# Second attention layer: the four product blocks of a sheet issued in three groups instead of four

## The reference, cut to what matters

```python
for ci in range(n_chunks):                      # chunks of 64 queries
    s = ci * chunk_size
    e = min(s + chunk_size, T)
    scores = jnp.einsum('bhtd,bhsd->bhts', q[:, :, s:e], k[:, :, :e]) * scale
    probs = jax.nn.softmax(scores, axis=-1)
    ...
    probs = probs * (0.5 + 0.5 * fhn_gate)      # a gate from the row's sum of probabilities
    probs = probs / (probs.sum(axis=-1, keepdims=True) + 1e-08)
    out_chunks.append(jnp.einsum('bhts,bhsd->bhtd', probs, v[:, :, :e]))
```

## Time and profile before

| | us |
|---|---|
| median of 3 runs | 1532.0 (1529.15 to 1532.43) |
| the profiled execution, its own time | 1530.86 |
| its span, first to last instruction | 1529.0 |
| second layer's stage, from the first scores (L2004) | 816.1 to the end |
| TensorE matmul busy | 1415.1 (93%) |
| VectorE busy | 1179.3 (77%) |
| ScalarE busy | 818.9 (54%) |
| GpSimd busy | 524.4 (34%) |

### The profile page before, as it was taken

How to read it: one execution, slowest core, us unless ns; L and a number is a source line. 1 busy time by engine, 2 the same in 40 slices (tenths; PEclk the granted TensorE clock), 3 DMA queues, 4 the chain that set the end, 5 groups by cost and what they waited for, 6 DMA issues and landing times.

```text
span 1529.0 us, 35462 instructions
## 1 busy us (share of the span) xinstructions
PE 1415.1 (93%) x12938; PEld 914.1 (60%) x12952; DVE 1179.3 (77%) x2690; ACT 818.9 (54%) x1565; POOL 524.4 (34%) x943
## 2 busy tenths in 40 slices
PE   3899999999998799999998999999999999999994
PEld 1667667667677699998885444444444444444432
DVE  3899889889888496456677788888888888888752
ACT  2344434534533333334434677777667777776672
POOL 2343333333233011162412244444444444442121
PEclk8899999999998899999999999999999999999996
DMA  4111111111111566776974343343344443432300
GB/s 121 40 42 56 47 40 58 45 42 56 38 37 36 160 211 209 213 249 209 269 201 78 91 104 99 93 105 93 85 102 105 103 101 94 104 89 71 81 9 14
DMA packets 119084, 152.86 MB, mean 100 GB/s; under 512 B 31348, under 2 KB 83700, under 8 KB 114292
## 3 DMA queue, kind: packets, MB, share of 16 engines
q1 hardware_dynamic: 105992, 120.25, 28.9%
q0 software_dynamic: 12928, 30.43, 6.9%
HBM read 109.01 MB, written 41.09 MB: 98 GB/s over the span
## 4 chain that ended last, share of the span: by engine, by line
PE 49%; DVE 32%; POOL 6%; issue 5%; ACT 5%; SPq 2%; DMA 1%; POOLq 0%; DVEq 0%; ACTq 0%
PE bank L1935 8%; PE bank L1926 8%; DVE P L1198 8%; DVE nmax L1503 8%; PE bank L1803 5%; PE bank L1981 5%; PE bank L2004 4%; ACT P L939 3%; PE bank L1760 2%; PE bank L1837 2%; PE bank L1944 2%; PE bank L1851 2%; DVE t L1073 1%; DVE t L1071 1%; PE bank L2051 1%
## 5 line engine op out<-in xcount | busy, mean ns | idle before, releaser
L1503 DVE TENSOR_REDUCE nmax<-bank 128x1 f32<-128x512 f32 (+3 forms) x704 | 428.6, 633 | 87.7 <-PE bank L1981 86.9
L939 ACT ACTIVATE P<-bank 128x512 f32<-128x512 f32 x640 | 371.3, 599 | 186.0 <-PE bank L2004 179.8
L1981 PE MATMUL bank<-KT,QT 76*128 76x512 bf16 (+3 forms) x1024 | 252.2, 304 | 28.8 <-DVE nmax L1503 20.4
L2004 PE MATMUL bank<-QT,KT 78*128 78x512 bf16 (+3 forms) x1024 | 246.1, 303 | 9.0 <-ACT P L939 5.6
L687 POOL DMA_INDIRECT xs_d<-xn,idx x128 | 124.5, 972 | 308.0 <-PE bank L1760 218.5
L1981 PEld LDWEIGHTS bank<-KT,QT 76*128 76x128 bf16 x1024 | 87.4, 97 | 188.2 <-DVE nmax L1503 129.4
L1803 PE MATMUL bank<-P,V 128*32 128x512 f32 (+3 forms) x2048 | 193.1, 450 | 0.0
L1198 DVE TENSOR_TENSOR P<-bank,early_w 128x512 f32<-128x512 f32 x256 | 158.6, 680 | 37.9 <-PE bank L1760 37.8
L903 ACT ACTIVATE hr<-bank 128x512 f32<-128x512 f32 x144 | 86.0, 597 | 177.9 <-PE bank L1926 174.9
L735 POOL DMA_INDIRECT hT<-ys_d,idx x104 | 103.5, 995 | 162.4 <-PE bank L2004 133.8
L1467 DVE TENSOR_TENSOR hT<-hr 128x512 f32<-128x512 f32 x144 | 98.0, 691 | 68.3 <-ACT hr L903 67.6
(11 more groups left out here) (257 smaller groups left out, 2227.2 us busy)
## 6 DMA issues: line engine op xcount, KB each, us to landing
P<-in_fc SPq DMA_DIRECT2D x72, 256.0 KB, 2.9
P<-in_proj SPq DMA_DIRECT2D x72, 256.0 KB, 3.5
QT<-parts_d SPq DMA_DIRECT2D x96, 192.0 KB
parts_d<-parts SPq DMA_DIRECT2D x32, 384.0 KB, 2.7
P<-xs_d SPq DMA_DIRECT2D x72, 128.0 KB, 3.0
ys_d<-P POOLq DMA_DIRECT2D x72, 128.0 KB, 3.6
KT<-parts_d SPq DMA_DIRECT2D x64, 128.0 KB
KT<-parts_d SPq DMA_DIRECT2D x32, 192.0 KB
```

Source lines behind the costliest of these rows:

```text
L939: nc.scalar.activation(P[s % 2][:, u, :], bank[k % 2][:, :], ACT.Exp, scale=float(DH) ** -0.5).then_inc(s_sb, 1)
L1503: nc.vector.tensor_reduce(nmax[:, s // TWO, h:h + TWO * nh - 1:TWO, j], max_bank(n, k)[:, 0:nh * w].rearrange("p (h w) -> p h w", h=nh), A ...
L1981: ins = pe.matmul(max_bank(n, k)[:, i * w:(i + 1) * w], QT[n.p][0:MROWS, h, j * 128:(j + 1) * 128], KT[n.p][0:MROWS, h, 0:w], start=True, ...
L2004: ins = pe.matmul(bank[k % 2][:, c:c + n], KT[b.p][0:SROWS, h, 128 * kb:128 * kb + 128], QT[b.p][0:SROWS, h, 128 * kb:T], start=True, stop ...
```

## The change

Three of the four blocks move or stay as follows: k = 0 stays behind unit 1, k = 1 goes from unit 3 to unit 4, k = 2 goes from unit 5 to unit 7, directly ahead of k = 3, which stays. Same instructions, same order among the blocks, same waits.

```diff
@@ -89,6 +89,7 @@
 PV_ORDER = [(0, G), (1, 2 * G), (3, 2 * G), (2, UNITS)]
+PV_AT = {1: (0,), 4: (1,), 7: (2, 3)}
 PLACE = {(g, kb): (u, c) for u in range(UNITS) for g, kb, c in unit_parts(u)}
@@ -2107,10 +2108,11 @@
                         maxes(2 if u == EXTRA else 1)
                         if core:
                             shifted_scores(b, s, u)
-                        if u in (1, 3, 5, 7) and s == 0 and before_:
-                            pv(b + -1, SHEETS - 1, u // 2)
-                        if u in (1, 3, 5, 7) and s > 0 and core:
-                            pv(b, s - 1, u // 2)
+                        for k in PV_AT.get(u, ()):
+                            if s == 0 and before_:
+                                pv(b + -1, SHEETS - 1, k)
+                            if s > 0 and core:
+                                pv(b, s - 1, k)
                         if where == (0, 1) and core:
                             r_rows(b)
```

## The result

The changed kernel takes 1548.11 us (median of 4 runs, 1547.29 to 1552.64), the kernel before 1532.22 (4 runs, 1529.15 to 1533.01). The ratio is 1.0116, 95% interval 1.0095 to 1.0138. The medians lie 15.9 us apart; by the ratio it is 17.8 us (14.6 to 21.1). Forecast was 1538.5, 6.5 us above the kernel before, and 1543.5 was the upper end. The direction was right; the forecast rise was less than half of the measured one.

What follows compares the result with a forecast made beforehand. A closed loop per batch passes between GpSimd's gate chain, VectorE, TensorE and ScalarE; 0.22 us in pass 0 plus 0.27 in pass 1 over 13 batches, plus ends, made 7.1 us: 1538.5 us, +0.4%, range 1531.5 to 1543.5.

Steps and rivals of the forecast that it cites:

- The price of a block: TensorE's product blocks: 0.21 us per 128 columns plus constants 0.14 and 0.09; joined pair taken at 0.79 us, at most 0.93.
- rival 4: Joined blocks: joining saves nothing, giving the upper bound of 1543.5 us; counted inside the main case, no chance of its own.
- k = 2 leaves unit 5, k = 1 goes to unit 4 in pass 1: Pass 1: -0.45 us for k = 2, a new 0.50 us stall at unit 4's second maximum for k = 1.
- k = 2 joins k = 3, pass 0: Block behind unit 7 grows by 0.22 us, delaying ScalarE's copy, the exponential of (0,8) and the scores of (1,0).
- Pass 2: Beside GpSimd's gate chain, covered by 1.30 us of slack: cost nothing, up to 0.3 us if that cover were gone.
- Period: Time per batch: 44.07 us instead of 43.58, from 0.22 in pass 0 plus 0.27 in pass 1.
- The whole part: Total of the summed terms over all batches: 13 x 0.49 = 6.4 us, 7.1 with first and last batches.
- Every sign that I had named for the changed profile: Joined block 0.79 us to next start, 0.5 us wait at (1,4), copy 0.22 later, tanh 0.49 later, batch 44.07.
- Pass 3: (3,5) and (3,6) delayed by 0.7 and 0.3 us, unnoticed by full VectorE; cost 0 to 0.1 us, taken as 0.
- so no term below is one of clock: All four passes: TensorE's granted clock is 1.00, its upper level of 2.4 GHz, so no clock term was counted.
- The bounds: Whole kernel: upper 1543.5 us with the joined pair at 0.93; lower about 1535 with the unit 4 stall at 0.25.
- The first rival: TensorE bounds throughout, each of 64 joined pairs returns 0.23 us: -14.7 us, 1517, or 1529 from pass 1 only; chance 0.12.

Runs made afterwards that it cites:

- e10: Kernel before, with k = 2 moved from unit 5 to unit 7 in pass 3 alone, k = 1 left behind unit 3; ratio 1.0050 to the kernel before.
- e3: Kernel before, with k = 2 joined to k = 3 behind unit 7 in all passes, k = 1 left behind unit 3; ratio 1.0031 to the kernel before.
- e1: Changed kernel with pass 3 alone put back as before; ratio 1.0038 to the kernel before.
- e2: Kernel before with pass 3 alone as in the changed kernel; ratio 1.0043 to the kernel before.
- e5: Changed kernel with the matmul of the first maximum of (3,4) issued five times, four matmuls more per batch; ratio 1.0025 to the kernel before.
- e11: Kernel before, with k = 1 moved from unit 3 to unit 4 in pass 3 alone, k = 2 left behind unit 5; ratio 1.0180 to the kernel before.
- e4: Kernel before, with k = 1 moved from unit 3 to unit 4 in all passes, nothing joined; ratio 1.0124 to the kernel before.
- e6: Kernel before, with k = 1 moved to unit 4 in pass 0, k = 2 joined to k = 3 in pass 1; ratio 0.9945 to the kernel before.
- e7: As e6, with the matmul of the first maximum of (3,4) issued three times; ratio 0.9985 to the kernel before.

## Why the prediction was right in direction and wrong in size

*The price of a block*: right. 0.79 us for the joined pair (1106.37 to 1107.16 in the changed kernel, 1182.81 to 1183.60 in e10); rival 4 falls.

*k = 2 leaves unit 5, k = 1 goes to unit 4 in pass 1*: right. Predicted a stall of 0.50 and +0.27 in pass 1; measured 0.51 and +0.29 ((1,3) to (1,8) of the changed kernel, 0.43 - 0.14).

*k = 2 joins k = 3, pass 0*: +0.22 predicted for joining, +0.22 measured (e3); in the changed kernel +0.14, because the moved k = 1 gives 0.08 ahead of it, a term that I left out.

*Pass 2*: right, beside the gate's chain; VectorE's idle time behind GpSimd went from 1.30 to 1.20 us.

*Period*: 44.07 predicted, 44.05 measured. That close is partly luck: 0.08 too much in pass 0, 0.02 too little in pass 1 and 0.04 more between (1,8) and (3,1), which I had at nothing, nearly cancel. The whole part, 7.1 us in the sum, measured 5.8 by the ratio (3.2 to 8.3, e1). Every sign that I had named for the changed profile came, and none of them looked at the clock.

*Pass 3*: the step that failed, with the sentence at its head, that the clock was 1.00 in all passes, "so no term below is one of clock". I walked pass 3 for delays alone, and these were right: (3,5) and (3,6) come 0.73 and 0.23 us later in e2, 0.7 and 0.3 were forecast. The wait at (3,4) is there in the working ("waits for VectorE anyway, 0.57 us"), not that it would grow, and I costed it at nothing since VectorE leads. It does cost nothing in time at full clock (e2: 43.58). But it moved 0.79 us of TensorE's work out of a stretch in which the engine was already waiting, its wait grew from 0.57 to 1.06 us with another 0.27 ahead of it, and in five of twelve batches the granted clock then fell to 0.50. At half clock TensorE becomes the bound of pass 3: 10.3 of the 15.7 us. The bounds had no such term, so the range ended at 1543.5. e1 takes the falls away by undoing pass 3 alone, e2 brings them back by changing pass 3 alone, and e5 has none after giving TensorE work in the wait without undoing the change.

*The first rival*, and with it the Trainium skill's rule (TensorEngine Tiling (Array Packing), Key Properties, changing the tiling mode drains TensorE): the trace agrees that a change of form costs about 0.23 us, and e3's pass 1 gained 0.28 from one pair fewer. What it does not give is the time of the kernel: of four passes only pass 1 can cash it.

What stays open: why the fall comes in some batches (every second in e2, every third from batch 1 on in e11) and not in each, when the undisturbed batches are alike to a few hundredths of a us; why e4 showed one fall and e11, with the same pass 3, four; why e6 gains more than its period; and how much of e5's gain over the changed kernel is the chip's.

## What to carry to other kernels

Work that fills an engine's wait is not free to move, even if the wait is on nobody's path: before moving matmuls out of a stretch in which TensorE already idles, add up what TensorE still does there, and carry a fall of the clock as a term of its own in the range. A granted clock of 1.00 before the change, as here, is no promise that it stays. Place work per stage, not by one rule for all: joining gained 0.28 us in pass 1 and lost 0.22 in pass 0, moving gained 0.08 in pass 0 and lost 0.57 in pass 1, and of the placements tried only a choice pass by pass (e6, e7) beat the kernel before.

## What the runs showed of the hardware that I had not expected

A kernel with four more matmuls in each batch was some 14 us faster against its kernel before (1.0025 instead of 1.0116, on two sets of rounds), and its granted clock stayed at 1.00 in batches 1 to 13. And moving 0.36 us of work out of a stretch that TensorE does not bound (e10) brought two falls of 6.8 us, 2.6 us each, in a kernel whose undisturbed batches took 43.58 us as before.
